# Turning the gate logits by transposes, and the gate products of batch 1 in one block of 512 tokens

## What is computed

```python
x = x + fake_quant(layernorm(x)) @ fake_quant(ctx)            # per batch, 512x1024 @ 1024x1024
h = layernorm(x)
ratio = mean(|h[153:]|) / mean(|h[:153]|)                     # per batch
logits = concat(h, ratio) @ gate_w + gate_b                   # 3 experts
scores = softmax(logits); top_val, top_idx = top_k(scores, 2); top_val /= sum(top_val) + 1e-8
x = x + sum_i top_val[..., i] * expert(top_idx[:, 0, i])(h)   # expert: act(h @ w1 + b1) @ w2 + b2
```

## Time and profile before

| what | value |
|---|---|
| median of 3 runs | 405.59 us |
| lowest and highest run | 405.22, 408.02 us |
| the profiled execution, its own time | 405.39 us |
| its span, first to last instruction | 403.6 us |
| mean granted TensorE clock | 0.999 |
| PE busy, DVE busy, ACT busy | 96%, 82%, 49% of the span |

### The profile page before, as it was taken

One profiled execution on the slowest core, in us unless ns is written; L12 is line 12 of the kernel. 1 busy time (PEld: TensorE's weight loads), 2 busy tenths in 40 slices (PEclk: granted clock), 3 DMA queues, 4 the chain that ended last, 5 costly groups with the idle time before them and its releaser, 6 DMA issues.

```text
span 403.6 us, 5336 instructions
## 1 busy us (share of the span) xinstructions
PE 388.8 (96%) x1932; PEld 306.9 (76%) x1932; DVE 329.3 (82%) x512; ACT 196.2 (49%) x254; POOL 57.5 (14%) x78
## 2 busy tenths in 40 slices
PE   2998979999999999999999999999999999999996
PEld 2435736888888888888888888888888888888885
DVE  8799876488999788897899996596998865949983
ACT  3578554174347633661826455343476333425720
POOL 8748400000000003482100004000000000000000
PEclk9999999999999999999999999999999999999999
DMA  8993039523006586000000499600045870000112
GB/s 313 412 408 120 2 121 373 186 76 133 2 0 192 175 286 233 2 0 2 0 2 0 133 367 378 218 0 0 2 159 206 251 263 8 2 0 1 54 52 104
DMA packets 23325, 52.82 MB, mean 131 GB/s; under 512 B 1760, under 2 KB 1792, under 8 KB 23296
## 3 DMA queue, kind: packets, MB, share of 16 engines
q1 hardware_dynamic: 22592, 50.34, 35.0%
q0 software_dynamic: 640, 2.10, 1.5%
q10 hardware_dynamic: 64, 0.02, 0.0%
HBM read 48.26 MB, written 4.19 MB: 130 GB/s over the span
## 4 chain that ended last, share of the span: by engine, by line
PE 94%; DVE 3%; ACT 1%; DMA 1%; issue 0%; POOL 0%; POOLq 0%; DVEq 0%; ACTq 0%
PE ps L1577 43%; PE ps L1549 38%; PE ps L1343 7%; PE ps L1389 2%; PE ps L1375 2%; DMA xres<-in_x_dram 1%; PE ps L1352 1%; DVE bn L788 1%; ACT q1T L569 1%; PE ps L1410 1%; DVE xres L859 0%; PE ps L1275 0%; ACT q L526 0%; PE ps L1331 0%; PE ps L1316 0%
## 5 line engine op out<-in xcount | busy, mean ns | idle before, releaser
L634 ACT ACTIVATE w_hi<-raw 128x1024 fp32r<-128x1024 f32 x88 | 88.5, 1053 | 44.7 <-DVE raw L985 22.5
L954 DVE TENSOR_TENSOR w_lo<-raw,w_hi 128x1024 fp32r<-128x1024 f32 x88 | 103.3, 1217 | 2.2 <-ACT w_hi L634 1.9
L1577 PE MATMUL ps<-hT_hi,w_hi 128*128 128x512 f32 x256 | 99.9, 390 | 0.0
L1577 PE MATMUL ps<-hT_lo,w_hi 128*128 128x512 f32 x256 | 99.6, 389 | 0.0
L1577 PE MATMUL ps<-hT_hi,w_lo 128*128 128x512 f32 x256 | 99.6, 389 | 0.0
L1549 PE MATMUL ps<-w_hi,a_hi 128*128 128x512 f32 x224 | 87.6, 391 | 0.0
L1549 PE MATMUL ps<-w_hi,a_lo 128*128 128x512 f32 x224 | 87.2, 389 | 0.0
L1549 PE MATMUL ps<-w_lo,a_hi 128*128 128x512 f32 x224 | 87.2, 389 | 0.0
L722 ACT ACTIVATE act_f<-ps,b1T 128x512 f32<-128x512 f32 x32 | 22.0, 689 | 103.6 <-PE ps L1577 103.6
L1577 PEld LDWEIGHTS ps<-hT_hi,w_hi 128*128 128x128 f32 x256 | 48.1, 188 | 10.1 <-issue 0.2
L1577 PEld LDWEIGHTS ps<-hT_hi,w_lo 128*128 128x128 f32 x256 | 48.1, 188 | 10.0
(11 more groups left out here) (153 smaller groups left out, 375.9 us busy)
## 6 DMA issues: line engine op xcount, KB each, us to landing
raw<-in_L_ffn_w_dram SPq DMA_DIRECT2D x64, 512.0 KB, 5.5
raw<-in_ctx_dram SPq DMA_DIRECT2D x16, 512.0 KB, 11.6
xres<-in_x_dram SPq DMA_DIRECT2D x8, 512.0 KB, 9.6
b2row<-in_L_ffn_b_dram SPq DMA_DIRECT2D x4, 512.0 KB, 6.6
out_dram<-xres POOLq DMA_DIRECT2D x8, 256.0 KB, 8.0
out_dram<-xres SPq DMA_DIRECT2D x8, 256.0 KB, 2.0
small<-in_L_xattn_x_scale_dram ACTq DMA_DIRECT2D x2, 0.0 KB
small<-in_L_xattn_x_zp_dram ACTq DMA_DIRECT2D x2, 0.0 KB
```

The source lines that it names most:

```text
L634: nc.scalar.activation(w_hi[n % SLOTS][:, 2 * c:2 * c + 2, :], region(q)[:, 2 * c:2 * c + 2, :], ACT.Copy).then_inc(w_hi_ready, 1)
L954: V.tensor_tensor(w_lo[n % SLOTS][:, 2 * c:2 * c + 2, :], region(n % QUARTERS)[:, 2 * c:2 * c + 2, :], w_hi[n % SLOTS][:, 2 * c:2 * c + 2, ...
L1577: last = T.matmul(ps[:, G1_BANK + f % 2, :], w[q % SLOTS][:, k % TT, fs], h[:, k, :], start=n == 0, stop=n == 3 * KT - 1)
```

## The change

Two edits. First, `gate_turn` transposes each tile of `lgT` (8 x 128) by the 8 x 8 identity to 128 x 8 in place of multiplying it by `pick_logit`, for both batches; `choose_scores` adds the bias to the high parts and then the low parts by one more DVE instruction, with its own wait; `pick_logit` and the instruction that made it (L1093) go. Second, for batch 1 alone, the four `gate_product(1, t)` are replaced by one `gate_products(1)` behind product (3, 1), 16 matmuls of 512 columns. Batch 0 keeps `gate_product`.

```diff
             def choose_scores(b):
 
                 dve.wait_ge(logit_ps, b + 1)
-                lps = ps[:, TURN_BANK[b], 0:4 * TT].rearrange("p (t e) -> p e t", e=4)
+                turned = ps[:, TURN_BANK[b], 0:8 * TT].rearrange("p (t h e) -> p h e t", h=2, e=4)
                 for e in range(NE):
-                    last = V.tensor_scalar(sc[:, e, :], lps[:, e, :], gbias[:, e:e + 1], None, ALU.add)
+                    last = V.tensor_scalar(sc[:, e, :], turned[:, 0, e, :], gbias[:, e:e + 1], None, ALU.add)
                 then(last)
+                then(V.tensor_tensor(sc[:], sc[:], turned[:, 1, 0:NE, :], ALU.add))
...
-                V.tensor_reduce(pick_logit[:], ident[0:8, 0:8].rearrange("p (h e) -> p e h", h=2), AX.X, ALU.add)
...
+            def gate_products(b):
+
+                pe.wait_ge(hT_lo_ready, 2 * TT * (b + 1))
+                n = 0
+                for k in range(KT):
+                    for h in (hT_hi, hT_lo):
+                        last = T.matmul(ps[0:8, LOGIT_BANK, :], gw_parts[:, k, :], h[:, k, :],
+                                        start=n == 0, stop=n == 2 * KT - 1)
+                        n += 1
+                last.then_inc(logitT_ps, 1)
...
                 for t in range(TT):
-                    last = T.matmul(ps[:, TURN_BANK[b], 4 * t:4 * t + 4], lgT[:, t * P:(t + 1) * P], pick_logit[:],
-                                    start=True, stop=True)
+                    last = T.transpose(ps[:, TURN_BANK[b], 8 * t:8 * t + 8], lgT[:, t * P:(t + 1) * P],
+                                       ident[0:8, 0:8])
                 last.then_inc(logit_ps, 1)
...
                             if (i, j) == (0, 1):
                                 transpose_h(1, 2)
-                                gate_product(1, 0)
                                 sum_abs(1)
-                            elif (i, j) == (1, 1):
-                                gate_product(1, 1)
                             elif (i, j) == (2, 1):
                                 transpose_h(1, 3)
-                                gate_product(1, 2)
                             elif (i, j) == (3, 1):
-                                gate_product(1, 3)
+                                gate_products(1)
                             elif (i, j) == (4, 0):
                                 gate_turn(1)
```

More of the change, by code:

```diff
@@ L171, in build @@
         classes = sb("classes", [P, 4], F32)
-        pick_logit = sb("pick_logit", [8, 4], F32)
         tm = sb("tm", [P, 8], F32)
```

## The result

The changed kernel takes 407.30 us, the median of 20 runs (406.71 to 408.48). The kernel before, run beside it, takes 406.14 (20 runs). The ratio is 1.0031, with a 95% interval of 1.0021 to 1.0041, which is 0.85 to 1.67 us of 406.14. Within 1% that is no change, but it is a loss, and the forecast of 405.8 (range to 407.0) was too low.

A forecast was written before the change was run, and what follows sets the result against it. PE was taken to bound the kernel, with DVE setting the end around batch 0's turn and nearly full in batch 1. Terms -0.28 - 0.54 - 0.19 + 1.44 = +0.43 on 405.39 gave 405.8 us, range 404.0 to 407.0.

The forecast's parts named there:

- the base: Start of the sum: the profiled execution's 405.39 us, with the median of the runs, 405.59, taken as 0.2 higher.
- Batch 0: Batch 0's turn: transposes save 0.48 us, the added DVE instruction costs 0.20, sum -0.28 us on the chain.
- The turn in batch 1: Batch 1's turn on PE's path: four transposes in 0.44 us in place of 0.98, so -0.54 us.
- Batch 0 gives nothing: Rival, batch 0's turn: another engine is there at the same time, or the addition costs 0.49; 406.1 us, chance 0.08.
- The block: Batch 1's gate product as 16 matmuls of 512 columns: 3.63 us in place of about 3.82, so -0.19 us.
- The wait at product (3, 0): Batch 1, p = 1: PE arrives early and waits for DVE's first `w_lo` chunk, starting at 211.52; +1.44 us.
- no wait opens: Rival, batch 1: DVE's queue moves along with PE, so PE doesn't stall; 404.4 us, chance 0.15.
- the one with two matmuls for a transpose: Rival, both turns: each transpose stays two matmuls, so the turn isn't shortened; 406.8 us, chance 0.05.
- the one with the clock: Rival, product (3, 0): after over 1 us of rest PE's clock is halved for 24 matmuls; 411.3 us, chance 0.03.
- PE's busy time was to fall by about 1.0 us: Expected sign in the profile after: PE's busy time falls by about 1.0 us, its idle time rises by about 1.4.
- L1093, one small instruction in a DVE queue at 9.5 us, I cost at nothing: Start of the kernel: removing this DVE instruction counts as nothing, at most its own 0.1 us.

The follow-up runs named there:

- c1_after: The changed kernel run once more with no edit, compared with the kernel before: ratio 1.0014 [0.9998, 1.0030].
- e6_bias_later: The changed kernel with batch 1's `router_bias` moved behind the `w_lo` quarter that product (3, 0) needs, in DVE's order: 406.02 us, ratio 0.9989.
- e11_time: The changed kernel with DVE's L1091 widened from 128 x 16 to 128 x 128 elements, no instruction added: ratio 1.0021.
- e3_tile_reduce: The changed kernel with the `pick_logit` tile and its instruction put back, read by nothing: 406.60 us, ratio 1.0007.
- e8_wait: The changed kernel with one more, long-met wait in DVE's stream where L1093 stood: ratio 1.0007.

## Why the prediction was right and wrong

**Result.** Forecast +0.43 us on the profiled 405.39. The stages that the change touches, with the one that I left out, give +0.83, and the runs +1.16 between the medians. About 0.3 of that remains beyond the sum; it is at the edge of the interval (0.85), and c1_after, the same kernel again, gave 0.57 by its ratio (-0.08 to 1.22) and 1.00 by its medians, so I take it for spread. The rest of the distance to 407.3 is the base: 405.39, and the median of three shown, 405.59, lay 0.75 and 0.55 below the 406.14 that 20 runs give.

**Batch 0: right in kind, too small.** -0.28 forecast, -0.43 measured. The transposes took 0.43 from end to end, not 0.58, and the addition 0.18 with 0.02 ahead of it, as assumed.

**The turn in batch 1: right.** x4 in place of x8, 0.34 us against 0.44 forecast. The rate of 0.109 came from transposes with 128 columns; these have 8. The Trainium skill ("TensorE: Matmul & The Clock Gate", Terms) calls the transpose mode four times faster for fp32. Here 0.98 became 0.34, 2.9 times, so the trace lies between the rule (0.25) and my row (0.44). With 0.43 for batch 0, the rival "Batch 0 gives nothing" fell as well.

**The block: right.** 3.63 forecast, 3.69 to 3.70 measured. That is 0.231 each, the upper of the two rates in the earlier trace rows, so that weights of 8 columns didn't help.

**The wait at product (3, 0): right in place, cause and time.** Forecast: PE's real start at 211.52, after DVE's first `w_lo` chunk, with 0.14 from one to the other. Measured: 213.53, with DVE shifted by 2.00 against before (207.77 to 209.77 for `result(1, 1)`, and the like); 211.52 + 2.00 is 213.52. The stage has +0.60 where the terms -0.54, -0.19 and +1.44 gave +0.71, and the block alone +1.23. e6_bias_later settled the cause: the wait vanished with an edit to DVE's order alone. The rival "no wait opens" fell, and so did the one with two matmuls for a transpose, and the one with the clock: 1.03 us of rest behind transposes cost nothing more, product (3, 0) took 5.69 where e6_bias_later, without the rest, has 5.67. One sign was not borne out: PE's busy time was to fall by about 1.0 us and fell by 0.1 (388.8 to 388.7). The long matmuls of the start-up hide it, L1343's group being 1.4 us busier (31.6 to 33.0).

**The step that failed: "L1093, one small instruction in a DVE queue at 9.5 us, I cost at nothing: at most its own 0.1 us".** It cost 0.66 us, and with the other sign: the kernel got slower by taking it out. I had bounded the edit by the instruction's duration. The runs show that its duration counts for nothing here (e11_time), and its being there for 0.66 (e3_tile_reduce, e8_wait), by way of a pause of DVE's ahead of tile 5's statistics and a longer q_rstd of POOL's behind it. Why DVE pauses stays open. The reason that I gave, "since PE's and ACT's work of the attention follows it on the chain", was a misreading: the chain names one way, and DVE's and POOL's way to the transposes was only some 0.05 us behind PE's, so nothing hid the loss. No row of the kernel before could have told where the pause would fall, though POOL's `hbuf` at 31.90 could have told that the stage had no slack for one. But the range had room for such a loss only if I had given "an instruction is taken from a DVE queue on the path" a price from both sides, as I did for the others.

**A second term was mis-sized: the base.** I added +0.43 to the 405.39 of one execution, and gave its distance from a typical one 0.2 us, from three runs. 20 runs have 0.75. Neither error alone takes the time out of the range: 407.30 - 0.66 is 406.64, and 407.30 - 0.75 is 406.55. It took both.

## What to carry to other kernels

Work that is moved on the bounding engine from ahead of a wait to behind it, where the wait is for a second engine that is itself full, isn't saved: the engine arrives early, waits, and does the work afterwards (the block alone cost 1.23 us). So list that engine's fixed times first, and take out only as much as their slack allows (here two of the four tiles, and the stage gained 0.80 us in place of losing 0.60). When several small parts are changed at once, split the profiles by marks that lie on the path, and ask of each stage whether its difference has a cause in the diff. A difference under 1 us between two profiled executions says nothing until the start-up is taken out of it, and one instruction more or less in a queue can cost or give more than its own time. A chain that names one engine doesn't say how far behind it the next way is: look up when the other engines' inputs to the same instruction were ready.

## What I had not expected of the hardware

- Removing one DVE instruction of 0.15 us made the stage behind it 0.66 us longer, and one wait that never waits took it away (30.30 to 29.62 us). It was the same in all 14 profiles: 29.60 to 29.64 with as many instructions ahead as before, 30.29 to 30.32 with one fewer. No packet of instructions started in the pause.
- One and the same POOL instruction took 0.72 us in the six profiles in which it began within 0.02 us of a DVE instruction, and 1.01 in the eight in which it began 0.3 us into that instruction. That the one makes the other isn't shown.
- Matmuls of 128x512 in f16 took 0.63 us each at first and 0.38 from then on, with the granted clock shown at full speed throughout. The last long one began anywhere from 12.8 to 17.0 us into the span, and the first mark moved with it by up to 2 us between the profiles.
- Four fp32 transposes of 8 x 128 took 0.34 us where the products had taken 0.98, as one matmul each in place of two. A matmul with only 8 weight columns took 0.231 us for 512 columns, no less than one with 128.
